# Moving the sort arithmetic of the context rows from period -1 to period 0, spreading its scatters over six later periods, and loading the context rows earlier

## The chip, the cores and the metric

One core of one Trainium2 chip. The metric is the device time of one execution, in microseconds. Five engines work side by side and meet at semaphores: TensorE (PE, its weight loads PEld), VectorE (DVE), ScalarE (ACT), GpSimd (POOL) and SyncE (SP), which only issues transfers. "Queue" rows (SPq, POOLq) are the issuing side.

## The reference

A decoder layer on 16 batches of 128 rows of width 128, in float32:

```
x = x + attn(LN(x))           # causal local attention, 16 heads of 8
x = x + cross(LN(x), ctx)     # cross attention; K and V rows of ctx by the row's bucket (8 buckets)
x = x + ffn_block(LN(x))      # multi-head attention, LN, mixture of 8 experts, LN
```

The part that matters here: K = ctx[row] @ Wk[bucket[row]] and V likewise. The kernel sorts the 2048 context rows by bucket into 23 tiles of 128 rows, multiplies each tile by its bucket's weights, stores the products and gathers them back.

## The kernel before, in words

32 tiles go through one software pipeline: tiles 0 to 15 are the batches of the first attention, 16 to 31 those of the cross attention. `PERIODS` is -4 to 38. Each engine has its own written-out loop over the periods, and an engine works strictly in the order written. In period p PE takes `scores_by_key(p)` (L1274), `less_max(p)` (L1284), `turn_xn(p+3)` (L1218), `weighted_sum(p-1)` (L1328), `turn_max(p+1)` (L1210), `project_qkv(p+3)`, `scores_by_query(p+2)` (L1311). In the same period DVE takes `maxima(p+1)` (L487, L490), `keys_by_head(p+2)` (L463), `norm_stats` to `norm_variance` of tile p+4 (L440 to L452), `queries_by_head(p+1)` (L463) and `norm_rows(p+4)` (L458), with POOL's `norm_power(p+4)` (L837) between the last two. ACT exponentiates the scores of tile p in four groups (`exp_group`, L969), and between the first and the second of them it copies the turned rows of tile p+3 (`turn_xn`, L950), for which PE's `turn_max` and `project_qkv` wait.

The sorting runs beside this:

- DVE: `bucket_hots` in period -3; PE: `count_buckets` in period -2; then DVE's `bucket_tiles` (L535 to L542) at the head of period -1, ahead of `maxima(0)`, and `bucket_slots` (L546 to L554) inside period -1, ahead of `norm_rows(3)`. `slot_i` (L550) says to which sorted row each context row goes, `tile_bucket` (L554) which weights a tile takes.
- POOL: `scatter_ctx(b)` (L845), one indirect transfer for each of the 16 batches: in periods -1 to 4, behind that period's `norm_power`, 4, 3, 3, 2, 2, 2 of them. The first waits for the context rows (`ctx_in`), the zeroed sorted rows (`zero_rows`) and `slots_ready`. `pad_masks` (L870, L872) follows in period 4.
- SP: after `buckets_ready` the first eight weight tiles, and after all 16 scatters (`scattered`, L347) the sorted rows in three loads (L349 to L352).
- PE: `turn_sorted(0)` (L1388) in period 6 waits for the first of these loads (`sorted_in`); `sorted_kv` (L1399) follows, and so on until period 11. ACT's `copy_sorted(0)` stands ahead of the last two `exp_group` of period 6.
- DVE's `cross_masks(b)` (L561, L563) runs in period b + 5; SP sends the masks on in groups of four batches (L324, L325).

At the start SP issues the first batch, `w_qkv` and batches 1 to 3, waits for the constants that ACT's queue loads (`heads_in`, `sort_in`, `consts_in`), and then issues the context rows (L277), the zeroing of the sorted rows (L279) and batches 4 to 15 (L281), in that order.

Of the kernel before, what the change touches and what calls it, by code (L numbers as in the profile page):

```python
# [23 lines left out]
    return 0 <= t < T  # L24


SCATTERS = (range(0, 4), range(4, 7), range(7, 10), range(10, 12), range(12, 14), range(14, 16))
SORT_TILES = 23
SORT_GROUP = 4
SORT_GROUPS = 6  # L30
# [12 lines left out]
def decoder_kernel(nc, x, ctx, fside, fsideT, itokT, pad, padT, w_qkv, w_out, wq, wkv, wo, bo,  # L43
# [10 lines left out]
    with st:  # L54
# [215 lines left out]
        def _(sp):  # L270
            sp.dma_start(x_sb[:, 0:1, :], x[0:1].rearrange("b s d -> s b d")).then_inc(s["x_in"], 16)
            sp.dma_start(w_qkv_sb[:, :], w_qkv).then_inc(s["wqkv_in"], 16)
            sp.dma_start(x_sb[:, 1:4, :], x[1:4].rearrange("b s d -> s b d")).then_inc(s["x_more_in"], 16)
            sp.wait_ge(s["heads_in"], 16)
            sp.wait_ge(s["sort_in"], 48)
            sp.wait_ge(s["consts_in"], 32)
            sp.dma_start(ctx_sb[:, :, :], ctx.rearrange("b s d -> s b d")).then_inc(s["ctx_in"], 16)  # L277
            sp.wait_ge(s["zeros_ready"], 1)
            sp.dma_start(ctx_sorted.rearrange("(t p) d -> p t d", p=128),  # L279
                         zeros.unsqueeze(1).broadcast_to([128, SORT_TILES, D])).then_inc(s["zero_rows"], 16)  # L280
# [126 lines left out]
        def _(dve):  # L407
# [177 lines left out]
                                  ALU.subtract, ALU.mult).then_inc(s["y0_ready"], 1)  # L585

            for p in PERIODS:
                if p == -1:
                    bucket_tiles()
                if live(p + 1):  # L590
                    maxima(p + 1)
                if live(p + 2) and p != -1:
                    keys_by_head(p + 2)
                if live(p + 4) and p != -1:
                    norm_stats(p + 4)
                if live(p - 2):
                    divide(p - 2)
                if live(p + 4) and p != -1:
                    norm_aggregate(p + 4)
                    norm_variance(p + 4)  # L600
                if p == -4:
                    scale_wq()
                if live(p - 3):
                    residual(p - 3)
                if p == T - 2:
                    dve.wait_ge(s["ffn_w_in"], 16 * nloads[0])
                    dve.tensor_scalar(inw_sb[:, 0:D], inw_sb[:, 0:D], MHD ** -0.5, None, ALU.mult)\
                        .then_inc(s["w_ffq_ready"], 1)
                    dve.tensor_scalar(inb_col[:, 0:1], inb_col[:, 0:1], MHD ** -0.5, None, ALU.mult)\
                        .then_inc(s["w_ffq_ready"], 1)  # L610
                if live(p + 1):
                    queries_by_head(p + 1)
                if p == -1:
                    keys_by_head(1)
                    norm_stats(3)
                    norm_aggregate(3)
                    norm_variance(3)
                    bucket_slots()
                if 0 <= p - Y0_STATS < B:
                    y0_stats(p - Y0_STATS)  # L620
                if live(p + 4) and p != -1:
                    norm_rows(p + 4)
                if p == -3:
                    bucket_hots()
                if p == -2:
                    negative_pick()
                if p == -1:
                    norm_rows(3)
                if 0 <= p - Y0_STATS < B:
                    y0_variance(p - Y0_STATS)  # L630
                if 0 <= p - Y0_ROWS < B:
                    y0_rows(p - Y0_ROWS)
                if p == B - 4:
                    dve.wait_ge(s["xw_in"], 48)
                    dve.tensor_scalar(wq_sb[:, :], wq_sb[:, :], HD ** -0.5, None, ALU.mult)\
                       .then_inc(s["wq_ready"], 1)
                if 0 <= p - 5 < B:
                    cross_masks(p - 5)
                if p in QK_PERIODS:
                    mha_keys(QK_PERIODS.index(p))  # L640

# [188 lines left out]
        def _(pool):  # L830
# [49 lines left out]
            for p in PERIODS:  # L880
                if live(p + 4):
                    norm_power(p + 4)
                if 0 <= p - Y0_STATS < B:
                    y0_power(p - Y0_STATS)
                if -1 <= p < 5:
                    for b in SCATTERS[p + 1]:
                        scatter_ctx(b)
                if p == 4:
                    pad_masks()
                if SORT_FROM + SORT_GROUPS <= p < SORT_FROM + SORT_GROUPS + 8:  # L890
                    for b in range(2):
                        gather_kv(2 * (p - SORT_FROM - SORT_GROUPS) + b)
                if B <= p + 1 < T:
                    v_place(p + 1)
                if B <= p + 4 < T:
                    add_bo(p + 4)
                b = p - Y0_TURN - 1
                if 0 <= b < B:
                    if b == 0:
                        pool.wait_ge(s["ffn_w_in"], 16 * nloads[0])  # L900
                    pool.wait_ge(s["f_xT_done"], b + 1)
                    pool.tensor_tensor(x_sb[:, b, :], x_sb[:, b, :], ln_rows[:, 3, :], ALU.add)\
                        .then_inc(s["xb_ready"], 1)
                    pool.tensor_tensor(y0[:, b, :], y0[:, b, :], ob_rows[:, :], ALU.add).then_inc(s["y0_biased"], 1)
# [900 lines left out]
```

## Time and profile before

| | |
|---|---|
| median of 3 runs | 338.67 us (338.23 to 341.26) |
| profiled execution, its own time | 339.11 us |
| its span | 337.3 us |
| mean granted TensorE clock | 0.981 |
| PE busy | 319.2 us (95%) |
| DVE busy | 261.2 us (77%) |
| ACT busy | 166.6 us (49%) |
| POOL busy | 126.0 us (37%) |
| chain that ended last | PE 73%, DVE 10%, issue 8%, POOL 5%, ACT 1%, DMA 1% |

The table's busy times are averages over the span. The granted clock is the share of full speed that TensorE was given; 1.00 is 2.4 GHz and 0.50 is 1.2 GHz. Ends of matmuls are modelled in the profile, their starts are recorded.

### The profile page before, as it was taken

Reading aid. Unit: us, or ns where it says so; the run is one execution under the profiler, and the core shown is the slowest. Engines: PE = TensorE matmul, PEld = TensorE weight load, DVE = VectorE, ACT = ScalarE, POOL = GpSimd, SP = SyncE. Lnnn points to the kernel's source line nnn. Section 1 sums busy time; section 2 is a strip of 40 time slices with the busy share of each in tenths; the row PEclk is TensorE's granted clock in tenths of the full one; section 3 lists DMA queues with packets and bytes.
Section 4 is the critical chain, followed back from the end, with each engine's and each line's share of the span. In section 5 each row is a group of like instructions: output and inputs, shape, how many; then the busy total and the mean of one; then the engine's idle time right before and its main releaser. Section 6 shows DMA issues by size and latency. Waiting matters only on the chain.

```text
span 337.3 us, 12339 instructions
## 1 busy us (share of the span) xinstructions
PE 319.2 (95%) x4780; PEld 219.0 (65%) x4780; DVE 261.2 (77%) x661; ACT 166.6 (49%) x458; POOL 126.0 (37%) x208
## 2 busy tenths in 40 slices
PE   7869999999999999999999999999999999998994
PEld 3425556666666556565565665657666769898994
DVE  6874578866667789998899999875555638879996
ACT  2223545666666446455465564645425546733331
POOL 1063555100000254645423534234700005814896
PEclk9976999999999999999999999999999999999998
DMA  4972230636456163589556000000000000044412
GB/s 109 300 201 87 70 138 25 181 113 150 144 166 163 50 177 90 157 194 226 163 145 193 3 4 2 2 6 1 2 2 4 2 2 0 6 126 132 152 30 66
DMA packets 38697, 31.89 MB, mean 95 GB/s; under 512 B 4968, under 2 KB 36208, under 8 KB 38512
## 3 DMA queue, kind: packets, MB, share of 16 engines
q1 hardware_dynamic: 36064, 27.37, 28.9%
q0 software_dynamic: 1280, 3.15, 3.8%
q8 instruction: 39, 0.64, 0.8%
q10 hardware_dynamic: 1296, 0.59, 0.7%
q14 instruction: 18, 0.15, 0.1%
HBM read 23.40 MB, written 7.70 MB: 92 GB/s over the span
## 4 chain that ended last, share of the span: by engine, by line
PE 73%; DVE 10%; issue 8%; POOL 5%; ACT 1%; DMA 1%; POOLq 0%; DVEq 0%
PE ps L1328 9%; PE ps L1311 9%; PE ps L1274 8%; PE ps L1248 3%; PE ps L1227 3%; PE ps L1284 3%; PE ps L1361 3%; PE ps L1240 3%; PE ps L1399 3%; PE ps L1698 2%; PE ps L1344 2%; PE ps L1417 2%; PE ps L1218 2%; PE ps L1437 2%; POOL room L913 2%
## 5 line engine op out<-in xcount | busy, mean ns | idle before, releaser
L969 ACT ACTIVATE pT<-ps 128x512 f32<-128x512 f32 x128 | 73.9, 612 | 89.4 <-PE ps L1284 81.8
L837 POOL TENSOR_TENSOR rstd<-veps,minus_half 128x1 f32<-128x1 f32 x32 | 18.8, 586 | 117.2 <-DVE veps L452 117.1
L487 DVE TENSOR_REDUCE m_pad<-ps 128x8 f32<-128x1024 f32 x32 | 39.1, 1222 | 19.4 <-PE ps L1311 19.2
L463 DVE TENSOR_TENSOR p_sb<-qk_sb,heads 128x512 f32<-128x512 f32 x64 | 45.0, 705 | 0.9 <-ACT qk_sb L984 0.5
L490 DVE TENSOR_REDUCE m_pad<-ps 128x8 f32<-128x1024 f32 x32 | 38.9, 1216 | 0.0
L1274 PE MATMUL ps<-p_sb,qk_sb 32*128 32x512 f32 x256 | 38.1, 667 | 0.0
L1311 PE MATMUL ps<-p_sb,qk_sb 32*128 32x512 f32 x256 | 37.5, 656 | 0.0
L1328 PE MATMUL ps<-pT,p_sb 128*32 128x128 f32 x1024 | 35.1, 276 | 0.2 <-issue 0.2
L1284 PE MATMUL ps<-mT,negsel 32*128 32x128 f32 x512 | 33.0, 365 | 0.4 <-issue 0.4
L1698 PE MATMUL ps<-mexp,pT 128*128 128x128 f32 x256 | 31.9, 278 | 1.2 <-DVE pT L784 0.9
L1284 PEld LDWEIGHTS ps<-mT,negsel 32*128 32x128 f32 x512 | 21.3, 192 | 16.2 <-issue 16.2
L1698 PEld LDWEIGHTS ps<-mexp,pT 128*128 128x128 f32 x256 | 29.9, 192 | 2.0 <-DVE pT L784 1.8
L908 POOL TENSOR_TENSOR rs<-ve,half 128x2 f32<-128x2 f32 x15 | 12.2, 816 | 45.8 <-DVE ve L704 45.5
L1328 PEld LDWEIGHTS ps<-pT,p_sb 128*32 128x32 f32 x1024 | 26.3, 109 | 4.5 <-issue 1.0
L877 POOL TENSOR_TENSOR rs<-ve,half 128x1 f32<-128x1 f32 x16 | 9.3, 580 | 29.5 <-DVE ve L579 29.4
L845 POOL DMA_INDIRECT ctx_sorted<-ctx_sb,slot_i x16 | 16.9, 1058 | 5.6 <-issue 4.0
L852 POOL DMA_INDIRECT kv_sb<-kv_sorted,slot_i x16 | 16.4, 1024 | 3.9 <-issue 3.6
L509 DVE TENSOR_TENSOR x_sb<-x_sb,ps 128x128 f32<-128x128 f32 x32 | 9.2, 287 | 9.5 <-PE ps L1361 8.8
L1240 PEld LDWEIGHTS ps<-causal,ident_bf 32*32 32x32 bf16 x512 | 4.5, 88 | 17.7 <-issue 10.7
L1240 PE MATMUL ps<-causal,ident_bf 32*32 32x512 bf16 x512 | 14.6, 405 | 1.3 <-DVE p_sb L463 0.9
L496 DVE RECIPROCAL rden<-ps 128x16 f32<-128x16 f32 x32 | 8.2, 257 | 9.4 <-PE ps L1227 9.3
L1274 PEld LDWEIGHTS ps<-p_sb,qk_sb 32*128 32x128 f32 x256 | 10.4, 190 | 7.7 <-issue 7.7
(203 smaller groups left out, 682.0 us busy)
## 6 DMA issues: line engine op xcount, KB each, us to landing
room<-mask_rows SPq DMA_DIRECT2D x32, 128.0 KB, 3.4
wkv_sb<-wkv SPq DMA_DIRECT2D x23, 128.0 KB
kv_sorted<-room SPq DMA_DIRECT2D x5, 512.0 KB, 3.1
w1t_sb<-w1t SPq DMA_DIRECT2D x8, 256.0 KB
w_sb<-w SPq DMA_DIRECT2D x8, 256.0 KB
kv_sb<-hot_rows SPq DMA_DIRECT2D x4, 512.0 KB, 5.4
ctx_sorted<-room SPq DMA_DIRECT2D x1, 1472.0 KB, 10.3
tk<-fside SPq DMA_DIRECT2D x1, 1024.0 KB
```

The costliest lines, as they stand in the source:

```text
L463: return dve.tensor_tensor(dst, rows.unsqueeze(1).broadcast_to([128, QUADS, S]), heads[:, 0, :].unsqueeze(2).broadcast_to([128, QUADS, S]) ...
L487: dve.tensor_reduce(m4[:, 0:2, 0:QUADS], ps[:, 0:2, :].rearrange("p g (j k) -> p g j k", j=QUADS), AX.X, ALU.max).then_inc(s["max_low"], 1)
L490: dve.tensor_reduce(m4[:, 2:4, 0:QUADS], ps[:, 2:4, :].rearrange("p g (j k) -> p g j k", j=QUADS), AX.X, ALU.max).then_inc(s["max_high"], 1)
L837: pool.tensor_tensor(rstd[:, :], veps[:, :], minus_half[:, :], ALU.pow)\
L845: pool.indirect_dma_start(ctx_sorted[:, :], bass.IndirectOffsetOnAxis(slot_i[:, b:b + 1], 0), ctx_sb[:, b, :], None).then_inc(s["scattered ...
L969: act.activation(pT[:, t % 2, g, :, :], quad[4 + g], ACT.Exp).then_inc(s["exped"], 1)
L1240: pe.matmul(quad[first + g][32 * c:32 * c + 32], ident_bf[group(g), group(g)], causal[group(g), side, c, :].unsqueeze(1).broadcast_to([32, ...
L1274: pe.matmul(quad[4 + g], keysT(t)[group(g)], qTm[group(g), t % 2, :, :], start=False, stop=False, skip_group_check=True)
L1284: mm = pe.matmul(quad[4 + g][:, j, :], negsel[group(g), j, :], mT[group(g), :], start=False, stop=True, skip_group_check=True)
L1311: pe.matmul(quad[g], qk_sb[group(g), t % 4, 0, :], kTm[group(g), t % 2, :, :], start=False, stop=True, skip_group_check=True)\
L1328: mm = pe.matmul(quad[1][32 * c:32 * c + 32, i, :], vaug[:, t % 4, h, :], pT[:, t % 2, h // 4, h % 4, :], start=(w == 0), stop=(w == 1), s ...
L1698: pe.matmul(dst, prod[:, b % 2, e, :], mexp[:, e, :], start=(e == 0), stop=False, skip_group_check=True)
```

## The change

In DVE's loop `bucket_tiles` and `bucket_slots` now run together in period 0, behind `norm_rows(4)`. The scatters run in periods 0 to 5 with 2, 3, 3, 3, 3, 2 of them. `pad_masks` moves from period 4 to 5, `cross_masks(b)` from period b + 5 to b + 6. SP issues the context rows ahead of its waits for the constants.

```diff
-SCATTERS = (range(0, 4), range(4, 7), range(7, 10), range(10, 12), range(12, 14), range(14, 16))
+SCATTERS = (range(0, 2), range(2, 5), range(5, 8), range(8, 11), range(11, 14), range(14, 16))
 ...
             sp.dma_start(x_sb[:, 1:4, :], ...)
+            sp.dma_start(ctx_sb[:, :, :], ctx.rearrange("b s d -> s b d")).then_inc(s["ctx_in"], 16)
             sp.wait_ge(s["heads_in"], 16)
             sp.wait_ge(s["sort_in"], 48)
             sp.wait_ge(s["consts_in"], 32)
-            sp.dma_start(ctx_sb[:, :, :], ctx.rearrange("b s d -> s b d")).then_inc(s["ctx_in"], 16)
 ...
             for p in PERIODS:
-                if p == -1:
-                    bucket_tiles()
                 if live(p + 1):
                     maxima(p + 1)
 ...
                     norm_variance(3)
-                    bucket_slots()
 ...
                     norm_rows(p + 4)
+                if p == 0:
+                    bucket_tiles()
+                    bucket_slots()
 ...
-                if 0 <= p - 5 < B:
-                    cross_masks(p - 5)
+                if 0 <= p - 6 < B:
+                    cross_masks(p - 6)
 ...
-                if -1 <= p < 5:
-                    for b in SCATTERS[p + 1]:
+                if 0 <= p < 6:
+                    for b in SCATTERS[p]:
                         scatter_ctx(b)
-                if p == 4:
+                if p == 5:
                     pad_masks()
```

## Rows read from the trace of the kernel before

**Rows 1.** Chain that ended last, 0 to 70 us: start, length, what.

```profile
21.44 3.03 issue
```

**Rows 2.** Busy time of each engine in stretches, with granted clock, DMA share, GB/s.

```profile
17.50:20.90 3.40, 3.40 (x44) 1.77 (x40) 3.12 (x8) 0.00 (x0) 1.62 (x2) 0.50 0.82 216
20.90:24.30 3.40, 0.43 (x5) 0.16 (x4) 2.27 (x6) 0.84 (x3) 2.76 (x4) 1.00 0.56 175
24.30:31.10 6.80, 6.58 (x59) 3.21 (x59) 2.16 (x3) 2.32 (x7) 3.38 (x4) 0.50 0.42 130
```

**Rows 3.** Instructions in order of time, tile 0's `less_max` and what follows.

```profile
19.36 1.71 PE L1284 MATMUL ps<-mT,negsel 32*128 32x128 f32 x16
...
21.77 1.09 POOL L845 DMA_INDIRECT ctx_sorted<-ctx_sb,slot_i  x1 [0.30 <-issue]
...
23.24 0.60 ACT L969 ACTIVATE pT<-ps 128x512 f32<-128x512 f32 x1 [7.61 <-remote]
```

**Rows 4.** DVE alone in the two stretches of the sort arithmetic.

```profile
11.00:12.56 1.56, 1.36 (x7) 1.00 1.06 291
16.64:18.65 2.01, 1.84 (x9) 0.71 1.12 329
```

**Rows 5.** DVE in order of time, `maxima(1)`, `norm_rows(4)` and `maxima(2)`.

```profile
19.08 1.23 DVE L487 TENSOR_REDUCE m_pad<-ps 128x8 f32<-128x1024 f32 x1 [0.17 <-issue]
...
24.77 0.40 DVE L458 TENSOR_SCALAR xn<-x_sb,mv,rstd 128x128 f32<-128x128 f32 x1 [1.53 <-POOL rstd L837]
29.34 1.23 DVE L487 TENSOR_REDUCE m_pad<-ps 128x8 f32<-128x1024 f32 x1 [4.17 <-PE ps L1311]
```

**Rows 6.** Scatters beside `less_max` and first exponentials, tiles 2 and 3.

```profile
36.55 0.85 PE L1284 MATMUL ps<-mT,negsel 32*128 32x128 f32 x11
36.94 0.96 POOL L845 DMA_INDIRECT ctx_sorted<-ctx_sb,slot_i  x1 [0.31 <-issue]
...
38.76 0.60 ACT L969 ACTIVATE pT<-ps 128x512 f32<-128x512 f32 x1 [3.53 <-PE ps L1284]
...
43.36 0.97 PE L1284 MATMUL ps<-mT,negsel 32*128 32x128 f32 x16
...
43.87 0.96 POOL L845 DMA_INDIRECT ctx_sorted<-ctx_sb,slot_i  x1 [0.30 <-issue]
...
45.36 0.60 ACT L969 ACTIVATE pT<-ps 128x512 f32<-128x512 f32 x1 [3.32 <-PE ps L1284]
```

**Rows 7.** Tile 4 with its first exponential, and `less_max` of tiles 5 and 6.

```profile
50.18 0.97 PE L1284 MATMUL ps<-mT,negsel 32*128 32x128 f32 x16
...
51.34 0.60 ACT L969 ACTIVATE pT<-ps 128x512 f32<-128x512 f32 x1 [2.51 <-PE ps L1284]
...
56.20 0.98 PE L1284 MATMUL ps<-mT,negsel 32*128 32x128 f32 x16
...
62.83 0.97 PE L1284 MATMUL ps<-mT,negsel 32*128 32x128 f32 x16
```

**Rows 8.** Last `norm_power` with scatters, sorted rows' load, their first use.

```profile
53.78 0.57 POOL L837 TENSOR_TENSOR rstd<-veps,minus_half 128x1 f32<-128x1 f32 x1 [2.78 <-DVE veps L452]
...
58.30 0.38 SPq L349 DMA_DIRECT2D room<-ctx_sorted  x1
...
60.57 0.57 POOL L837 TENSOR_TENSOR rstd<-veps,minus_half 128x1 f32<-128x1 f32 x1 [0.98 <-DVE veps L452]
...
65.50 0.60 PE L1388 MATMUL ps<-ident,room 128*128 128x128 f32 x4
```

**Rows 9.** DMA issues: size, median time from issue to landing.

```profile
room<-ctx_sorted SPq DMA_DIRECT2D x2, 256.0 KB, 3.1
```

**Rows 10.** SP's issue of batches 1 to 3, and the first use of the sort constants.

```profile
1.65 0.43 SPq L273 DMA_DIRECT2D x_sb<-x  x1
...
6.88 0.17 DVE L514 CAST room<-itokT_i 128x16 f32<-128x16 int32 x1
```

**Rows 11.** DMA issues again: the context rows.

```profile
ctx_sb<-ctx SPq DMA_DIRECT2D x1, 0.5 KB, 6.5
```

## The prediction

> **What bounds the kernel now.** PE works 95% of the span and its line is most of the chain of waits, so work taken from DVE or POOL counts only where PE stands still. I read the chain first, then the busy times by stretch, then the instructions in order around each hole. The largest hole of the first 70 us is PE's, 3.03 us behind tile 0's `less_max` [rows 1]. PE was busy 0.43 of those 3.4 us, and from 24.3 to 31.1 the granted clock is 0.50 (1.2 of 2.4 GHz), as it is from 17.5 to 20.9, before the hole [rows 2]. So the hole costs twice. What holds it is not DVE: `maxima(1)` begins at 19.08 and its two halves end at 21.44, where the hole begins. It is ACT's chain, whose first exponential starts at 23.24, although PE's last `less_max` work is drawn as done at 19.36 + 1.71 = 21.07 [rows 3]. Tile 4 shows the ordinary distance from the start of `less_max` to that exponential, 51.34 - 50.18 = 1.16 [rows 7]. Tiles 2 and 3 show 38.76 - 36.55 = 2.21 and 45.36 - 43.36 = 2.00, and in both a scatter starts 0.4 to 0.5 us into `less_max`, with ACT starting 0.86 and 0.53 us behind that scatter's end [rows 6]. Tile 0's exponential comes 0.38 us behind the end of a scatter too, 23.24 - (21.77 + 1.09) [rows 3]. I read this as one thing: a scatter on POOL that overlaps `less_max` keeps the matmuls' signals back until it is over, and the bunch of four in period -1, 0.3 us apart, kept tile 0's back for 23.24 - 21.07 = 2.2 us.
>
> **The arithmetic on DVE.** It takes 1.56 + 2.01 = 3.57 us where it stands [rows 4]. Both pieces stand ahead of maxima that PE waits for. Taken out, it lets `maxima(1)` start earlier than 19.08 [rows 5], by 0 (if PE's scores come no sooner) to 3.57; I take 1.7, about half, since the second piece alone is 2.01 and then the scores are waited for. That ends `maxima(1)` at 19.7. From there to `norm_rows(4)` DVE needs the 24.77 - 21.44 of before less 1.53 of waiting, 1.8 us, plus 0.3 that POOL's power still costs: 21.8, and 22.2 at its end [rows 5]. The moved 3.57 us follow and end at 25.7. Before, DVE had 4.17 us empty there, up to `maxima(2)` at 29.34 [rows 5]; now those scores should be ready by then, because the scatters are gone from tile 0 and the hole with them, and the arithmetic is itself what `maxima(2)` waits for. 29.34 - 25.7 = **3.6 us gained**. If the hole stays, the empty 4.17 us cover the 3.57 and nothing is gained or lost here. The clock was at half until 31.1, 1.8 us behind `maxima(2)`; at full it saves half of that, **0.9 us** (bounds 0 and 3.4, half of the whole 6.8 us).
>
> **The scatters that take their places.** `slot_i` is written three instructions before the arithmetic ends, so the two scatters of period 0 should fall into tile 1's `less_max`. Price: 0 to the 2.2 us of tile 0; nearest are the 2.21 - 1.16 = 1.05 and 0.84 of tiles 2 and 3 [rows 6, 7], and PE has other work queued for about half. I take **0.5 us lost**. Later, from one `less_max` to the next, it was 6.81 us for tile 2 (three scatters around it), 6.82 for tile 3 (two), 6.02 for tile 4 (two) and 6.63 for tile 5 (two and `pad_masks`) [rows 6, 7]. Now tiles 2 to 5 each have three. At 6.82 apiece they take 27.3 where they took 26.3: **1.0 us lost** (bounds: 6.02 apiece, 2.2 gained, and a second held signal in each, 2 lost). `pad_masks` goes to period 6, where it lies beside the wait of the next paragraph; without that wait it costs the 6.63 - 6.02 = 0.6 that it cost before.
>
> **The last scatters and PE's period 6.** Here the change adds a wait. The last two scatters now follow `norm_power(9)`, not `norm_power(8)`. From 53.78 to SP's load at 58.30 it was 4.5 us [rows 8], and the load lands 3.1 later [rows 9]. Counted from `norm_power(9)` at 60.57 the first sorted rows are there at 60.57 + 4.5 + 3.1 = 68.2; PE came to `turn_sorted(0)` at about 65.5 [rows 8]. All these move with PE, so the distance stays: 68.2 - 65.5 = 2.7, less 0.2 because in period 5 DVE ran late beside `pad_masks`. **2.5 us lost** (bounds 1.5 and 3.2). Behind that wait on PE stand the projections, `sorted_kv` and the scores; on ACT two exponentials stand behind `copy_sorted(0)`. Nothing in the order can fill it. The loads of the other sorted rows and the eight weight tiles have a period or more in hand. A hole of 2.5 us is near the one of 3.03 that was followed by half clock [rows 1, 2]. If the clock falls for a stretch like 17.5 to 20.9, half of 3.4, **1.7 us, is lost** (bounds 0 and the 3.4 of the longer stretch); I take the short one.
>
> **The rest.** `cross_masks` leaves period 5 for period 21, where DVE has two more norms to do: two operations, **0.4 us lost** (bounds 0 and 0.7). The masks go out one period later; SP then sends them 5 or 6 us later, always several periods ahead of their use, and the loads queued behind (expert weights, small weights) have as much in hand. The context rows' load is itself free: `zero_rows` and batches 4 to 15 come no later than before, as they follow in the same queue with 1 MB already moved. What it may cost is the constants beside it: DVE takes the sort constants at 6.88, before any context row is on its way; now the load goes out behind batches 1 to 3, at 1.65 + 0.43 = 2.1 [rows 10], and both travel together. I take 0 (bounds 0 and 1.7: were the constants late until the context rows land, 2.1 + 6.5 = 8.6 [rows 11], DVE would start its part 1.7 later).
>
> The Trainium skill speaks against this step (DMA: Bandwidth & Descriptors, Queues, rings and completion order). DMA engines take the queues in turn, but the increment that signals a transfer is written only after all earlier writes of that engine, from whatever queue. By that rule the constants' signals wait for context rows written before them, and the sum would be up to 1.7 us higher; no row of this trace has the two side by side.
>
> **The sum.** -3.6 - 0.9 + 0.5 + 1.0 + 2.5 + 1.7 + 0.4 = +1.6 us against the profiled execution's own 339.11, so 340.7. The median of the runs lies 0.44 below that execution: **340.3 us**. No change that can be told: about 1%, 3.4 us, is what a measurement of this kernel tells from none.
>
> **The rivals.**
> - The hole is not the scatters' (13%). ACT's row gives "remote" as the releaser [rows 3], no scatter, and from 24.3 to 31.1, with the next scatters beside it, PE was busy 6.58 of 6.80 us [rows 2]. Then PE's signals of tile 0 come as late as before, the start gains only about 0.4 us from the first maxima, and everything lost behind stays lost: -0.4 + 1.0 + 2.5 + 1.7 + 0.4 = +5.2, 343.9. It decides if the exponential still starts over 3 us behind the start of tile 0's `less_max`. For it: four scatters held back more than twice what one did. Against it: three tiles show the same 0.4 to 0.9 us behind a scatter's end.
> - Cheap later periods (20%). The clock holds through period 6 and bunches of three cost no more than those of two did: 1.6 - 1.7 - 1.0 = -1.1, 337.6. For it: 6.02 with two scatters. Against it: 6.81 with three.
> - Long half clock at period 6 (12%), as from 24.3 to 31.1: 1.7 more, 342.0.
> - Constants late (5%): +1.7, 342.0. For it: they share the DMA engines with 1 MB. Against it: the constants are small, and DVE asks for them only at 6.88 [rows 10].
> - The sorted rows are in time after all (5%), if POOL gets ahead of PE: no wait, no fall of the clock, 1.6 - 2.5 - 1.7 = -2.6, 336.1, and `pad_masks` then costs its 0.6, 336.7.
>
> **How the numbers follow.** Forecast 45%. Its own range is 337.5 to 342.5. For 8 in 10 I take in the first rival and most of the faster ones: 336.0 to 344.0. Faster by over 1% (below 335.3) needs the start's full gain and no wait in period 6, or a start that gains 6 or 7: 10%. Slower (above 342.1) is the first rival, half of the long half clock, and the tail of the forecast and of the late constants: 28%. The rest, 62%, is within 1%.
>
> **What the new profile would show.** No hole behind tile 0's `less_max`, with its first exponential within about 2 us of its start; DVE's arithmetic ending just where `maxima(2)` starts, with no empty time ahead of that; the clock at 1.00 from about 21 on; some 6.8 us from tile to tile for tiles 2 to 5; in period 6 PE waiting 2.5 us at L1388 for the load of the sorted rows, and half clock behind it. I am wrong if that first exponential stays late, if L1388 does not wait, or if waits appear that no part here names.

## The result: 1.0% slower, about 3 us

The changed kernel takes 341.03 us (median of 18 runs, 339.99 to 342.71), the kernel before beside it 338.24 (18 runs). The ratio, just inside the 1% that I call no change, is 1.0099, 95% interval 1.0075 to 1.0123; it compares the means of the fast runs, 341.07 and 337.74 us with one slow run of the kernel before left out, and these are 3.3 us apart where the medians are 2.8 apart. In a later group of runs it was 340.92 against 338.50, 1.0082 (1.0052 to 1.0112). So the forecast of 340.3 is 0.7 us low, and the time is in its range. Several steps behind it were wrong, and their errors cancelled in part: that the number came out is luck as much as reading.

The profiled execution of the changed kernel has a span of 340.8 us; at 342.71 us of its own it is the longest of the 18, so where its stages are priced below, the trace of a second execution (after_again) stands beside it. Read in order of time it answers to the rows of before one by one. First the start, which no row of before announced. One instruction per line: start, duration, engine, line, operands, idle time ahead and its releaser.

```profile
6.96 0.18 DVE L514 CAST room<-itokT_i 128x16 f32<-128x16 int32 x1
11.00 0.66 PE L1240 MATMUL ps<-causal,ident_bf 32*32 32x512 bf16 x16 [1.35 <-DMA ident_bf<-c_ident_bf]
11.59 2.09 PE L1311 MATMUL ps<-p_sb,qk_sb 32*128 32x512 f32 x8
13.74 1.23 DVE L487 TENSOR_REDUCE m_pad<-ps 128x8 f32<-128x1024 f32 x1 [3.12 <-PE ps L1311]
```

DVE takes the sort constants at 6.96, about as before [rows 10]. The last constants on ACT's queue come late: PE waits 1.35 us for `ident_bf`, and its scores run at half clock. SP stands behind the same constants: it issues the zeroing of the sorted rows at 11.03 (7.84 before). They land at 18.5, 0.4 us later than before, and batches 4 to 15 at 21.3, 0.9 later; nothing in this trace waits for either.

Then tile 0's `less_max`, the moved arithmetic (L535 to L554), and `maxima(2)`:

```profile
18.98 1.22 DVE L487 TENSOR_REDUCE m_pad<-ps 128x8 f32<-128x1024 f32 x1
19.71 0.97 PE L1284 MATMUL ps<-mT,negsel 32*128 32x128 f32 x16
20.70 0.60 ACT L969 ACTIVATE pT<-ps 128x512 f32<-128x512 f32 x1 [3.90 <-PE ps L1284]
...
23.58 0.34 DVE L458 TENSOR_SCALAR xn<-x_sb,mv,rstd 128x128 f32<-128x128 f32 x1 [0.43 <-POOL rstd L837]
23.84 0.28 DVE L535 TENSOR_TENSOR room<-room,sort_c 128x128 f32<-128x128 f32 x1
...
27.24 0.18 DVE L554 TENSOR_SCALAR tile_bucket<-room 128x24 int32<-128x24 f32 x1
27.33 1.22 DVE L487 TENSOR_REDUCE m_pad<-ps 128x8 f32<-128x1024 f32 x1
27.46 1.22 POOL L845 DMA_INDIRECT ctx_sorted<-ctx_sb,slot_i  x1 [3.92 <-DVE slot_i L550]
28.69 0.45 PE L1218 MATMUL ps<-ident,xn 128*128 128x128 f32 x1 [2.42 <-DVE m_pad L487]
```

Tile 0's first exponential is 20.70 - 19.71 = 0.99 us behind the start of `less_max`, where it was 3.88 [rows 3]: the old hole is gone. In its place PE waits 2.42 us for `maxima(2)`, which starts when the arithmetic ends and not before. The stretches show that this hole too is followed by half clock (window, length, busy time of PE, PEld, DVE, ACT, POOL with counts, granted clock, DMA share, GB/s):

```profile
10.90:14.30 3.40, 3.30 (x26) 1.05 (x27) 0.56 (x1) 0.18 (x1) 0.00 (x0) 0.50 0.70 194
14.30:28.00 13.70, 10.10 (x148) 5.19 (x146) 12.01 (x30) 4.41 (x13) 2.00 (x3) 1.00 0.49 126
28.00:34.80 6.80, 6.11 (x64) 3.69 (x64) 3.85 (x8) 2.94 (x8) 4.79 (x5) 0.50 0.47 128
34.80:69.00 34.20, 30.89 (x514) 18.55 (x510) 23.46 (x48) 15.48 (x44) 17.78 (x18) 1.00 0.24 80
69.00:76.00 7.00, 5.88 (x69) 4.02 (x72) 2.72 (x10) 4.08 (x10) 0.57 (x1) 1.00 0.77 223
```

Tile 3 is one of three that now have three scatters about their `less_max`:

```profile
41.81 1.10 POOL L845 DMA_INDIRECT ctx_sorted<-ctx_sb,slot_i  x1 [0.19 <-issue]
42.68 0.97 PE L1284 MATMUL ps<-mT,negsel 32*128 32x128 f32 x16
43.22 0.96 POOL L845 DMA_INDIRECT ctx_sorted<-ctx_sb,slot_i  x1 [0.30 <-issue]
44.48 1.26 POOL L845 DMA_INDIRECT ctx_sorted<-ctx_sb,slot_i  x1 [0.30 <-issue]
46.09 0.60 ACT L969 ACTIVATE pT<-ps 128x512 f32<-128x512 f32 x1 [4.71 <-remote]
```

Its exponential comes 3.41 us behind `less_max` (2.00 before), 0.35 behind the third scatter's end. In the chain of waits the holds of tiles 3 and 5 stand under a name of their own, as the profile finds no releaser on this core (start, length, what):

```profile
41.38 4.69 another core or an unknown queue
...
57.00 4.00 another core or an unknown queue
```

Last, period 6:

```profile
67.30 0.38 SPq L349 DMA_DIRECT2D room<-ctx_sorted  x1
70.17 0.65 PE L1388 MATMUL ps<-ident,room 128*128 128x128 f32 x4 [1.11 <-DMA room<-ctx_sorted]
```

The wait for the sorted rows is there, 1.11 us, and the clock stays at 1.00 (last stretch above).

### The profile page after: what moved, and what is told of

The parts are those of the page before. It is cut to its first block, busy times and chain, and to the rows that moved or that the text cites. A ratio compares the mean times of both kernels' runs of the same rounds, so it can differ in the third digit from the quotient of the medians.

```text
span 340.8 us, 12339 instructions
## 1 busy us (share of the span) xinstructions
PE 318.5 (93%) x4780; PEld 218.1 (64%) x4780; DVE 260.1 (76%) x661; ACT 166.3 (49%) x458; POOL 126.5 (37%) x208
## 4 chain that ended last, share of the span: by engine, by line
PE 73%; DVE 8%; POOL 5%; issue 4%; DMA 4%; another core or an unknown queue 3%; ACT 2%; ACTq 1%; POOLq 0%; DVEq 0%
PE ps L1311 9%; PE ps L1328 9%; PE ps L1274 8%; PE ps L1248 3%; PE ps L1284 3%; PE ps L1227 3%; PE ps L1399 3%; PE ps L1361 3%; PE ps L1240 2%; PE ps L1698 2%; PE ps L1417 2%; DMA ident_bf<-c_ident_bf 2%; PE ps L1437 2%; PE ps L1218 2%
## 5 line engine op out<-in xcount | busy, mean ns | idle before, releaser
L487 DVE TENSOR_REDUCE m_pad<-ps 128x8 f32<-128x1024 f32 x32 | 39.1, 1220 | 21.4 <-PE ps L1311 21.3
L463 DVE TENSOR_TENSOR p_sb<-qk_sb,heads 128x512 f32<-128x512 f32 x64 | 43.9, 687 | 0.1
L1328 PE MATMUL ps<-pT,p_sb 128*32 128x128 f32 x1024 | 37.5, 280 | 1.3 <-issue 1.2
L1274 PE MATMUL ps<-p_sb,qk_sb 32*128 32x512 f32 x256 | 36.5, 640 | 0.0
L1284 PE MATMUL ps<-mT,negsel 32*128 32x128 f32 x512 | 32.1, 357 | 0.7 <-issue 0.7
L1328 PEld LDWEIGHTS ps<-pT,p_sb 128*32 128x32 f32 x1024 | 27.4, 111 | 6.6 <-issue 3.1
L1240 PE MATMUL ps<-causal,ident_bf 32*32 32x512 bf16 x512 | 14.4, 398 | 2.2 <-DMA ident_bf<-c_ident_bf 1.4
L1240 PEld LDWEIGHTS ps<-causal,ident_bf 32*32 32x32 bf16 x512 | 4.5, 88 | 18.4 <-issue 11.1
```

The lines of the kernel that those rows point to most:

```text
L463: return dve.tensor_tensor(dst, rows.unsqueeze(1).broadcast_to([128, QUADS, S]), heads[:, 0, :].unsqueeze(2).broadcast_to([128, QUADS, S]) ...
L487: dve.tensor_reduce(m4[:, 0:2, 0:QUADS], ps[:, 0:2, :].rearrange("p g (j k) -> p g j k", j=QUADS), AX.X, ALU.max).then_inc(s["max_low"], 1)
L1240: pe.matmul(quad[first + g][32 * c:32 * c + 32], ident_bf[group(g), group(g)], causal[group(g), side, c, :].unsqueeze(1).broadcast_to([32, ...
L1274: pe.matmul(quad[4 + g], keysT(t)[group(g)], qTm[group(g), t % 2, :, :], start=False, stop=False, skip_group_check=True)
L1284: mm = pe.matmul(quad[4 + g][:, j, :], negsel[group(g), j, :], mT[group(g), :], start=False, stop=True, skip_group_check=True)
L1328: mm = pe.matmul(quad[1][32 * c:32 * c + 32, i, :], vaug[:, t % 4, h, :], pT[:, t % 2, h // 4, h % 4, :], start=(w == 0), stop=(w == 1), s ...
```

## Experiments

Five groups of runs were made, each with the kernel before beside it. Its median was 338.24, 337.36, 330.59, 338.50 and 330.29 us in groups 1 to 5. That it falls into two kinds became the main finding, so each result names its group. Only ratios within a group are compared.

To read all traces alike I took, from the instructions in order of time, the start of each tile's first L1274 operation. "Late" is the distance from the start of the tile's `less_max` to its first exponential. Five of the kernels have a line or two more, so that L1218 is L1219 or L1220 in them, and so on.

```
group kernel            t0     t1     t2     t6     t7     end    late, tiles 0 to 5
1  before             18.27  29.70  35.99  62.27  71.06  337.3  3.88 1.17 2.21 2.00 1.16 1.31
1  changed            19.15  24.74  35.42  65.29  75.78  340.8  0.99 0.99 1.05 3.41 2.35 2.68
2  ctx_back           17.81  23.40  32.78  62.86  73.28  338.1  0.99 0.99 2.15 3.44 2.33 2.69
2  scatters_later     17.90  25.74  31.33  60.46  73.09  338.7  0.99 0.99 2.92 2.91 1.84 1.88
2  two_each           19.23  24.81  35.51  60.30  72.86  337.2  0.99 0.99 0.99 2.04 1.16 1.34
2  no_scatters        17.89  23.47  34.47  59.58  69.27  333.8  0.99 in all
3  ctx_first          18.00  25.87  31.46  55.87  64.66  329.7  0.99 in all
3  before_gated       18.79  24.55  34.16  59.75  69.52  334.0  0.99 in all
3  split              17.96  23.55  29.89  53.69  66.35  331.5  0.99 in all
3  gated_slots_late   18.66  25.16  30.75  58.31  72.50  336.9  1.37, then 0.99
4  before_again       18.59  30.14  36.06  62.38  71.17  336.4  3.34 0.99 2.45 1.81 1.17 1.28
4  after_again        18.13  23.72  33.44  63.68  74.08  339.1  0.99 0.99 2.15 3.44 2.36 2.73
4  slots_late         18.81  24.52  39.60  69.57  78.36  344.4  0.99 1.60 0.99 3.43 2.31 2.65
5  counts_only        18.65  24.54  30.13  54.54  63.33  327.8  0.99 in all
```

The theories: S, a scatter on POOL beside `less_max` keeps TensorE's signals back; A, the early load makes constants late; B, the arithmetic holds up `maxima(2)`; and later D, such holds are there in some groups of runs only. The rivals stand in the expectations.

### The load back: ctx_back

```diff
             sp.wait_ge(s["consts_in"], 32)
+            sp.dma_start(ctx_sb[:, :, :], ctx...)   # moved back from ahead of the waits
```

> The changed kernel with one part undone: the context rows' load stands again behind SP's waits for the constants. Theory A (the constants were late because 1 MB of context rows travelled beside them): TensorE's operation at L1240, at 11.00 us in the changed kernel and 10.61 in the kernel before, starts again at 10.6 or a little before, maxima of tile 0 end the 1.2 us earlier that they did before, and tile 1's first less_max operation (24.74) comes about 0.9 us earlier; the whole is 0.9 us faster than the changed kernel, 1.007 of the kernel before. Rival (the first tile is late for the order of the loads on the queues, or by chance of the run): L1240 stays at 11.0 and the time is the changed kernel's.

Measured: 1.0102 (1.0053 to 1.0150), no faster than the changed kernel's 1.0099. The lateness itself is plain. `ident_bf` lands 7.2 us (7.1 in after_again) after its issue in the changed kernel and 2.8 here:

```profile
ident_bf<-c_ident_bf ACTq DMA_DIRECT2D x1, 32.0 KB, 2.8
```

But L1240 is due at 10.6 in any case and gets there at 10.61 here, so in a trace like this at most 0.4 us is left of the 4.4. In the changed kernel's profiled execution PE, at full clock until then, was free at 9.65 and did wait 1.35. Tile 0 stands 1.34 us earlier in this trace, and most of that is where the half clock fell: 7.8 to 11.2 here, 10.9 to 14.3 in the changed kernel. In after_again it fell at 8.1 to 11.6, and tile 0 came at 18.13 in spite of the late constants. A is right that the constants are late, and its price in the time is not resolved; the 0.9 us that it expected did not show.

### The load alone first: ctx_first

```diff
             sp.dma_start(x_sb[:, 1:4, :], ...)
+            sp.dma_start(ctx_sb[:, :, :], ctx...)
```

> The kernel before with the context rows' load alone moved up behind the first rows. Theory A (constants late): TensorE's L1240 starts at about 11.0 instead of 10.61, maxima of tile 0 end about 1.2 us later, tile 0's less_max follows 0.9 us later, and the whole is 0.9 to 1.3 us slower, 1.003 to 1.004 of the kernel before. Rival (the first two microseconds are taken up by later waits or by where the half clock falls): the late start shows in the trace, but the time is 1.000 of the kernel before, within 0.001.

Measured: 1.0012 (0.9995 to 1.0029), the kernel before at 330.59 us. `ident_bf` landed 6.6 us after issue, L1240 started at 10.61 without a wait. The rival is right on the time: the early load costs nothing that can be told. The late start that both expected did not show: `ident_bf` landed at 10.27, before PE came for it. But this trace held the surprise. It has the old order of scatters, and nothing is late:

```profile
18.56 0.98 PE L1284 MATMUL ps<-mT,negsel 32*128 32x128 f32 x16
18.86 1.22 POOL L845 DMA_INDIRECT ctx_sorted<-ctx_sb,slot_i  x1 [1.49 <-DMA ctx_sorted<-room]
19.55 0.60 ACT L969 ACTIVATE pT<-ps 128x512 f32<-128x512 f32 x1 [3.91 <-PE ps L1284]
```

### The new places of the scatters alone: scatters_later

```diff
 # the kernel before, with the change's SCATTERS, pad_masks, cross_masks;
 # bucket_tiles, bucket_slots and the load where they were
+                if 0 <= p < 6:
+                    for b in SCATTERS[p]:
```

> The kernel before with the new schedule of scatters, pads and cross masks alone; the arithmetic of slots and buckets and the context rows' load stay in their old places. Theory S (a scatter that overlaps less_max keeps its signals back): tile 0's first exponential starts about 1 us behind the start of its less_max, not the 3.9 of the kernel before, because no scatter is beside it; tile 1 has two beside it and is late by 1 to 2.5 us; tiles 3 to 5, with three each, lose about 3.7 us against the kernel before, as the changed kernel does, and period 6 loses 1.7. Start gain 4 less 5.4 lost: 1.000 to 1.008 of the kernel before. Rival P (the hole behind tile 0 comes from TensorE's own instruction supply or from the arithmetic ahead of maxima): the exponential still comes over 3 us behind, and the time is 1.015.

Measured: 1.0078 (1.0046 to 1.0109). This is the cleanest witness for S: from `maxima(0)` to 21 us DVE's instructions stand as before, within 0.1 us, and tile 0's lateness falls from 3.88 to 0.99 with no scatter beside it, while tiles 2 and 3 of the same trace, with scatters, are late by 2.92 and 2.91. One thing differs besides: tile 0's `less_max` ran at half clock before and at full clock here. That cannot make 3.88: in gated_slots_late `less_max` of tile 0 starts at half clock too, and the exponential follows after 1.37. Tile 1, expected late by 1 to 2.5, was not (0.99): its scatters had ended at 26.29, and its `less_max` began at 26.30. Tile 2 starts at 31.33, 4.7 us earlier. Tiles 2 to 5 then take 29.13 us instead of 26.28, and PE comes to period 6 early:

```profile
66.16 1.11 PE L1388 MATMUL ps<-ident,room 128*128 128x128 f32 x4 [2.30 <-DMA room<-ctx_sorted]
```

It waits 2.30 us, and the clock falls behind it:

```profile
65.90:69.30 3.40, 3.15 (x15) 3.15 (x16) 0.29 (x2) 1.57 (x3) 0.06 (x1) 0.50 1.00 279
```

The period takes 12.63 instead of 8.79: 3.8 us lost.

### Two scatters each: two_each

```diff
-SCATTERS = (range(0, 2), range(2, 5), range(5, 8), ...)
+SCATTERS = (range(0, 2), range(2, 4), range(4, 6), ..., range(10, 12))
-            sp.wait_ge(s["scattered"], 16 * B)
+            sp.wait_ge(s["scattered"], 16 * 12)
```

> The changed kernel with two scatters in each of six periods, so that batches 12 to 15 are not scattered at all (their rows are left out of the sorted context, and SP waits for twelve scatters). Theory S: with two in a period the second is over when less_max's last matmuls signal; the periods of tiles 3 to 5 (8.23, 7.44, 7.50 us in the changed kernel) come back to 6.0 to 6.8, together about 3.5 us faster than the changed kernel, 0.999 of the kernel before. Rival (the longer periods come from DVE being one tile late after the moved arithmetic, not from scatters): they stay at 7.4 to 8.2, and the time is within 0.5 us of the changed kernel's.

Measured: 1.0007 (0.9966 to 1.0047), without the rows of four batches. Tiles 3 to 5 take 6.86, 6.02 and 6.16 us instead of 8.23, 7.44 and 7.50: 4.1 us for the third scatter of each, and 4.1 as well against ctx_back in the same group. In tile 3 the exponential follows the second scatter's end:

```profile
41.83 0.97 PE L1284 MATMUL ps<-mT,negsel 32*128 32x128 f32 x16
42.36 0.96 POOL L845 DMA_INDIRECT ctx_sorted<-ctx_sb,slot_i  x1 [0.30 <-issue]
43.87 0.60 ACT L969 ACTIVATE pT<-ps 128x512 f32<-128x512 f32 x1 [3.34 <-PE ps L1284]
```

Some 2 us of it go again in period 6 (12.56 against 10.50), where PE now waits longer.

### No scatter: no_scatters

```diff
+SCATTERS = (range(0),) * 6
-            sp.wait_ge(s["scattered"], 16 * B)
+            sp.wait_ge(s["zero_rows"], 16)
 # and POOL waits for slots_ready ahead of its first gather
```

> The changed kernel with no scatter at all (the context rows are never put in sorted order; SP loads the zeroed rows, and POOL takes the slots first at the gathers). Bound of what the scatters cost in their new places. Theory S: every tile from 1 to 6 has its first exponential 1.0 to 1.3 us behind the start of less_max, no period over 6.9 us but that of tile 1, where the arithmetic still delays the maxima of tile 2; TensorE does not wait at L1388. About 7 us faster than the changed kernel, 0.988 of the kernel before. Rival: if the holes at tiles 3 to 5 stay without a scatter, they come from something else, and the time is within 2 us of the changed kernel's.

Measured: 0.9916 (0.9879 to 0.9953), 1.8% of the kernel before under the changed kernel. All tiles are at 0.99. So in this kind of group lateness and scatters go together throughout. Not every gap does: tile 4 takes 7.34 us (6.02 before), with PE standing 0.94 us at L1241 for nothing that the profile shows. Tile 1's long period stays, 10.99 us (with half clock from 26.5 to 34.0 in it), and so its cause is DVE (theory B), not a scatter:

```profile
26.54 0.18 DVE L554 TENSOR_SCALAR tile_bucket<-room 128x24 int32<-128x24 f32 x1
26.63 1.22 DVE L487 TENSOR_REDUCE m_pad<-ps 128x8 f32<-128x1024 f32 x1
...
27.99 0.45 PE L1219 MATMUL ps<-ident,xn 128*128 128x128 f32 x1 [2.99 <-DVE m_pad L487]
```

### The arithmetic in two places: split

```diff
 # the changed kernel, load back
+                if p == -1:
+                    bucket_tiles()
 ...
                 if p == 0:
-                    bucket_tiles()
                     bucket_slots()
```

> The changed kernel with the context rows' load back behind the constants and the arithmetic split: bucket_tiles (1.56 us) at the head of period -1 again, bucket_slots (2.01) behind norm_rows of tile 4 where the change has both. Theory B (tile 1's long period, 9.39 us with the load back, is DVE's arithmetic ending after maxima of tile 2 could have started, plus the half clock that follows): maxima of tile 2 start 1.5 us earlier against tile 1's less_max, PE's wait at L1218 falls from 2.4 to under 1 us, tile 1's period to 6 to 7.5 us, and bucket_tiles costs at most 1 us in period -1: about 1.5 us faster than with the arithmetic whole, 1.005 of the kernel before. Rival (the long period comes from the two scatters beside tile 1): it stays at 9 to 10 us.

Measured: 1.0077 (1.0053 to 1.0100), in a group where nothing was late. PE's wait at `maxima(2)` is 0.83 us, tile 1's period 6.35, the clock stays up, and `bucket_tiles` in period -1 costs nothing that shows (tile 0 at 17.96). B holds. The whole is slower than the 1.005 that was expected. What remains of the loss is period 6, 12.66 against 8.79 us in ctx_first:

```profile
59.37 1.11 PE L1389 MATMUL ps<-ident,room 128*128 128x128 f32 x4 [2.29 <-DMA room<-ctx_sorted]
```

```profile
59.20:62.60 3.40, 3.23 (x15) 3.23 (x16) 0.37 (x2) 1.58 (x4) 0.00 (x0) 0.50 1.13 298
```

### Scatters gated off less_max: before_gated and gated_slots_late

```diff
 # before_gated: the kernel before
+                    pool.wait_ge(sT_done[3], p + 2)
                     for b in SCATTERS[p + 1]:
 # gated_slots_late: also bucket_slots in period 0, scatters 4, 3, 3, 3, 3 in periods 0 to 4;
 # pad_masks and cross_masks stay where the kernel before has them
```

> The kernel before with one wait added: in each period -1 to 4 POOL begins its scatters only when TensorE's less_max of tile p+1 has signalled (semaphore sT_3 at p+2). Nothing else is moved: four scatters behind tile 0's less_max instead of beside it. Theory S (only a scatter that overlaps less_max keeps it back): tile 0's first exponential comes about 1.0 to 1.3 us behind the start of its less_max, and from tile 0's to tile 1's less_max it is about 7.8 us instead of 11.43; tiles 2 and 3 come to 6.0 to 6.1 from 6.8. Start and tiles together 4.5 to 5 us gained; 1 to 2 of them are lost again at L1388, as the last scatters start about 1.5 us later and TensorE is earlier: 0.990 of the kernel before. Rival C (the count of scatters in flight matters, not when they start): the hole only moves behind the gate, tile 0 to tile 1 stays over 10 us, and the time is 1.000. Rival P (TensorE's instruction supply or DVE's arithmetic makes the hole): the exponential still comes over 3 us late.

> The kernel before, with the load in its old place, bucket_tiles in period -1 and bucket_slots alone moved behind norm_rows of tile 4, the scatters in five periods (4, 3, 3, 3, 3, the last in period 4 as before), each bunch begun only when less_max of tile p+1 has signalled. By theories S and B together: no hole behind any less_max of tiles 0 to 5, tiles 1 to 5 at 6.0 to 6.5 us, TensorE about 5 us ahead of the kernel before at tile 6; then 1.5 to 2.5 us more wait at L1388 and perhaps 1.7 of half clock behind it: 334.5 to 336, 0.990 of the kernel before. Rival (POOL's three scatters from 1.1 us on end too late for the power of the next tile's norm, so DVE and the next maxima are late): tiles 2 to 5 at 6.8 us or more, and the time is 1.000.

Measured: 1.0140 (1.0115 to 1.0166) and 1.0192 (1.0149 to 1.0235), where 0.990 was expected of both. The group had no lateness to cure, so the gate had nothing to win there, and the rows show what it cost. Of before_gated:

```profile
25.38 0.96 POOL L845 DMA_INDIRECT ctx_sorted<-ctx_sb,slot_i  x1 [0.30 <-issue]
26.36 0.58 POOL L837 TENSOR_TENSOR rstd<-veps,minus_half 128x1 f32<-128x1 f32 x1
26.98 0.40 DVE L458 TENSOR_SCALAR xn<-x_sb,mv,rstd 128x128 f32<-128x128 f32 x1 [4.01 <-POOL rstd L837]
...
28.66 0.30 PE L1219 MATMUL ps<-ident,xn 128*128 128x128 f32 x1 [2.58 <-DVE m_pad L487]
```

POOL's next `norm_power` stands behind the delayed scatters, `norm_rows` waits for it, the maxima wait behind `norm_rows`, and PE for them. That is the mechanism of the rival in the second expectation, though not at the places that it named: in gated_slots_late tiles 3 to 5 take 6.0 to 6.2 us, and the loss sits in tile 2 (9.29, PE waiting 2.13 us for the maxima) and in period 6 (14.19, 2.98 us, with half clock from 61.5 to 68.5), where `pad_masks` too stands behind the gated scatters. Whether the gate would help where signals are held was not tried.

### The change again, and before: after_again and before_again

> The changed kernel once more, beside the kernel before on another chip. On the chip of the second group the scatters kept no less_max back (first exponential 0.99 us behind in every tile) and the kernel before took 330.6 us. Theory D (the hole behind tile 0's less_max, whose removal was the gain of the change, is there on some chips only): on a chip without it the change has nothing to gain at the start: tile 0 to tile 1 5.6 us instead of 7.9, tile 1 to tile 2 about 10 instead of 5.6, tiles 2 to 5 6.0 in both, period 6 12.7 instead of 8.8 with the wait at L1388 and half clock: 5 to 6 us slower, 1.015 to 1.018 of the kernel before. On a chip with the holes it is 1.010 again. Rival (the chips differ in speed alone, all by the same share): 1.010 on any chip.

> The kernel before once more, for its trace on the same chip as the two beside it. Theory D: where the time is about 330 us, tile 0's first exponential starts 1.0 us behind the start of its less_max although four scatters lie beside it, tile 0 to tile 1 takes about 7.9 us and tiles 2 and 3 take 5.7 to 6.0; where it is about 338 us, they take 11.4 and 6.8 as in the first trace. Rival: the shorter time is spread over all periods and the hole of tile 0 is there as well.

Measured: 1.0082 (1.0052 to 1.0112), and 338.33 us for one more run of the kernel before. It is a group with holds, and those of the first pair are there again (3.34 late in tile 0 before, 3.44 in tile 3 after); tile 2 is late by 2.15 this time, not 1.05. So the part of the expectation about a group without holds stays untested. By this pair the loss is in place at tile 7, 74.08 against 71.17; from there to the end both take the same, 265.0 and 265.2.

### The best guess: slots_late

```diff
 # the kernel before, pad_masks and cross_masks as in the change
-SCATTERS = (range(0, 4), range(4, 7), range(7, 10), range(10, 12), ...)
+SCATTERS = (range(0, 4), range(4, 7), range(7, 10), range(10, 13), range(13, 16))
-                    bucket_slots()            # period -1
+                if p == 0:
+                    bucket_slots()
```

> The kernel before with bucket_slots alone moved behind norm_rows of tile 4 (bucket_tiles stays at the head of period -1), the scatters in periods 0 to 4 (4, 3, 3, 3, 3), pad_masks and cross_masks one period later as in the change, the load of the context rows in its old place. The last scatters are in period 4 as before, so the sorted rows stay ahead of TensorE. Theory B: tile 0's period falls from 7.9 to 5.6 us, tile 1's rises from 5.6 to 6.4, period 6 stays at about 8.8 without a wait at L1388: 1 to 1.6 us faster on a chip without the holes, 0.996 of the kernel before. On a chip with the holes tile 0's hole goes (4 us gained) and bunches of three cost about 3: also 0.996. Rival (the sorted rows are late as in the change): a wait of 1 us or more at L1388, and 1.003.

Measured: 1.0245 (1.0198 to 1.0292), a miss by 9 us. No wait for the sorted rows, and period 6 takes 8.79, as theory B said. But seven scatters now follow one another, with one `norm_power` of 0.57 us between, and tile 1's period takes 15.08 us:

```profile
26.79 1.08 PE L1329 MATMUL ps<-pT,p_sb 128*32 128x128 f32 x32
26.85 0.96 POOL L846 DMA_INDIRECT ctx_sorted<-ctx_sb,slot_i  x1 [0.30 <-issue]
...
27.80 0.33 PE L1211 MATMUL ps<-ident,m_pad 128*128 128x128 f32 x1
...
29.65 0.41 PE L1346 MATMUL ps<-w_qkv_sb,xnT 128*128 128x128 f32 x2 [0.35 <-issue]
...
33.73 0.96 POOL L846 DMA_INDIRECT ctx_sorted<-ctx_sb,slot_i  x1 [0.31 <-issue]
...
35.61 0.37 ACT L976 COPY oT<-ps 128x256 f32<-128x256 f32 x1 [7.67 <-remote]
35.88 0.27 ACT L958 CAST mT<-ps 128x128 fp32r<-128x128 f32 x1
36.41 0.66 PE L1241 MATMUL ps<-causal,ident_bf 32*32 32x512 bf16 x16 [6.35 <-ACT mT L958]
```

ACT stands 7.67 us for the weighted sums (L976), which PE began at 26.79, and gets them at 35.61, 0.9 us behind the last scatter's end. The maxima that PE turned at 27.80 are next in ACT's order and are copied at 35.88, so of their own signal this says nothing; PE in turn waits 6.35 us for that copy. `less_max` of that tile was late by 1.60 alone. So what is held is not `less_max` in particular: here it is the signal of the weighted sums, and it stays held while scatters follow each other.

### The counts alone: counts_only

```diff
-SCATTERS = (range(0, 4), range(4, 7), range(7, 10), range(10, 12), range(12, 14), range(14, 16))
+SCATTERS = (range(0, 2), range(2, 5), range(5, 8), range(8, 11), range(11, 14), range(14, 16))
```

> The kernel before with the counts of the scatters alone changed: 2, 3, 3, 3, 3, 2 in periods -1 to 4 instead of 4, 3, 3, 2, 2, 2. No arithmetic, load, pad or mask is moved, and the last scatters stay in period 4. Theory E (on chips where TensorE's signals are held, what is held grows with the number of scatters in an unbroken run on POOL): two beside tile 0 hold its first exponential back by 1 us instead of 2.4 to 2.9, so tile 0's period falls from 11.5 to about 9; three beside tiles 3 and 4 lengthen these from 6.8 and 6.0 to 8.2 and 7.4, as in the changed kernel; period 6 stays 8.8 without a wait. Sum about 0, 0.997 to 1.003 of the kernel before. On a chip where nothing is held (the kernel before at about 330 us) nothing changes at all, 1.000. Rival F (only the overlap with less_max counts, not the number): tile 0's exponential is as late as with four.

Measured: 1.0002 (0.9989 to 1.0014), the kernel before at 330.29. It answers the second half of the expectation: where nothing is held, three in a bunch cost nothing. Tile 4 here, beside tile 3 of the changed kernel above:

```profile
42.31 0.96 POOL L845 DMA_INDIRECT ctx_sorted<-ctx_sb,slot_i  x1 [0.30 <-issue]
42.45 0.98 PE L1284 MATMUL ps<-mT,negsel 32*128 32x128 f32 x16
43.44 0.60 ACT L969 ACTIVATE pT<-ps 128x512 f32<-128x512 f32 x1 [2.34 <-PE ps L1284]
```

Theory E, that a hold grows with the unbroken run, was not put to the test by it. It rests on one scatter more giving 1.4 us more lateness in tile 3 (3.41 and 2.04), and on the seven of slots_late.

## Why the prediction came out, step by step

Measured beside the forecast, from the table: the first pair, then the second pair of the same kernels.

```
step                                      forecast   group 1   group 4
start to tile 2 (-3.6, -0.9, +0.5)          -4.0       -0.6      -2.6
tiles 2 to 5, bunches of three              +1.0       +3.6      +3.9
period 6, wait and half clock               +4.2       +1.7      +1.6
behind it (cross_masks)                     +0.4       -1.2      -0.2
end of the trace                            +1.6       +3.5      +2.7
```

**The hole behind tile 0 was the scatters'.** Right for groups of this kind, and the rival that denied it is out: scatters_later takes the hole away with no other order changed near it. Tile 0 to tile 1 fell from 11.43 to 5.59 us. Where nothing is held the hole is not there to be won: ctx_first has four scatters in the old place and takes 7.88.

**Where the arithmetic ends, and what follows it.** Wrong, the step that failed first, in two parts. The smaller is the end of the arithmetic: I put it at 25.7, and it was 27.4 in the profiled execution, because `norm_rows(4)` starts at 23.58 instead of the 21.8 that I reckoned. `maxima(1)`, which I let start at 17.4, started at 18.98, as the first tile was late by then, and that is 1.6 of the 1.8 us. This part belongs to that one execution: in after_again `maxima(1)` starts at 17.97 and in ctx_back at 17.64, close to the forecast. So `maxima(2)` came 2.0 us earlier in the first pair and 3.1 in the second (26.62 against 29.76), of the 3.6 forecast. The larger part holds in both: I took what `maxima(2)` gains for what tile 2 gains, and 0.9 us more for a full clock. But PE, relieved of one hole, now stands waiting for `maxima(2)`, 2.42 us at L1218 (2.73 in after_again), and half clock follows, to 34.8 (to 32.0). From `maxima(2)` to tile 2 it takes 8.09 us instead of 6.65, and 6.82 instead of 6.30 in the second pair: a loss of 1.4 and 0.5 where the forecast had a gain of 0.9. no_scatters has the same hole without any scatter, split all but removes it.

**Bunches of three.** The term that was most mis-sized, 1.0 forecast and 3.6 to 3.9 measured. I took the 6.82 of a tile with two as the price of three, after I had seen 2.2 us held by four. two_each prices the third scatter directly: 4.1 us over three tiles. The outer bound, a second hold in each, was 2 us and too small as well.

**Period 6.** The wait is where I put it. Its 2.5 us and the 1.7 of half clock are nearly what scatters_later (2.30, period +3.8) and split (2.29, period +3.9) show, where PE arrives on time. In the changed kernel PE came later than that, waited 1.11 (0.99 in after_again), and the clock held; forecast were 2.5 and a fall of the clock. By the rows the bunches kept PE back: tile 5 is late by 2.68 there and by 1.88 in scatters_later, which has bunches of three too. That this alone makes the difference between the two waits is argued, not tried. If it does, two errors here were one: what the bunches cost, the last wait gave back in part. I had priced them as independent terms, with "the distance stays".

**The constants.** I had asked the wrong ones. DVE's sort constants were in time; the last of ACT's queue landed 7.2 us after issue instead of 3.1. There 288 KB of constants travel beside 1 MB of context rows, and `ident_bf` lands 6.6 to 7.3 us after its issue in every kernel that loads early, 2.6 to 3.1 in every other. The Trainium skill (DMA: Bandwidth & Descriptors, Queues, rings and completion order) has the rule that a transfer's signal is written only after the earlier writes of that DMA engine, from whatever queue. The traces agree with it, and as well with a mere sharing of the DMA engines, which no run here tells apart from it. The lateness cost the time little, 1.0012 in ctx_first, where PE needed them only at 10.6. So the rival that I gave 5% was right on the lateness and wrong on its price and on who would wait. That zeroing and batches would come "no later than before" was wrong by 0.4 and 0.9 us, without a cost that shows.

**cross_masks.** Forecast 0.4 and not resolved; the pairs differ behind tile 7 by 0.2 to 1.2 us in the changed kernel's favour, and the first trace of before is the odd one there (266.2 us; 265.0 to 265.2 in the other three).

**The signs named beforehand.** The first exponential, the arithmetic ending where `maxima(2)` starts, and a wait at L1388 came as said. The clock at 1.00 from 21 on, 6.8 us a tile (it was 6.7 to 8.2) and half clock behind L1388 did not. Waits "that no part here names" were one of my signs of being wrong, and two are there: PE's for `ident_bf` and PE's at L1218.

## What to carry to other kernels

Filling a hole by moving work pays only up to the next thing that the relieved engine will then ask for, so after taking a hole away follow that engine forward to its next wait, not the mover. Waits in series on one engine can share their slack: price them together, since what one adds the next may give back. And where one kernel's median moves by over 2% from one group of runs to the next, look for a mechanism in the two traces before tuning for either.

## What the runs showed of the hardware

**TensorE's signals can be held while POOL issues indirect DMAs, in some groups of runs and not in others.** In groups 1, 2 and 4, with the kernel before at 337.4 to 338.5 us, the late exponentials came 0.1 to 1.1 us behind the end of a scatter. In groups 3 and 5, at 330.3 to 330.6, they came 0.99 us behind `less_max` with the same scatters beside it. That is most of the 8 us between the groups: from tile 0 to tile 7 the kernel before takes 52.6 us in before_again; its nearest kin of the other kind take 46.7 (ctx_first) and 44.7 (counts_only), for the kernel before itself has no trace there. Groups 4 and 5 ran on chips with the same number, so the number alone does not tell the kinds apart. What does, I can't say. Nor can I say how the signal comes to be late. It is not only that the operation starts late: in slots_late PE's matmuls of 29.65 had started 6 us before ACT got the weighted sums of 26.79. But operations are seen to start late too. In the changed kernel's tile 3 the matmuls behind `less_max` start in small lots with gaps, and the profile shows nothing that they wait for:

```profile
43.84 0.52 PE L1328 MATMUL ps<-pT,p_sb 128*32 128x128 f32 x9
44.54 0.42 PE L1328 MATMUL ps<-pT,p_sb 128*32 128x128 f32 x4 [0.18 <-issue]
45.26 0.42 PE L1328 MATMUL ps<-pT,p_sb 128*32 128x128 f32 x4 [0.30 <-issue]
45.98 0.68 PE L1328 MATMUL ps<-pT,p_sb 128*32 128x128 f32 x15 [0.30 <-issue]
```

**What the change would cost where nothing is held stays open.** An estimate from rows: tile 1 with the hole at `maxima(2)` takes 9.39 us in ctx_back and 10.99 in no_scatters, which has the longer half clock, and 5.59 in ctx_first. That is 3.8 to 5.4 lost, less the 2.3 gained in tile 0 (7.88 to 5.59), and 3.9 in period 6: 5.4 to 7.0 us, or 1.016 to 1.021 of 330.6. No run has it, and no version that I tried and that does the whole work beats the kernel before.
